# Seven products per group in another order, in a Winograd-form fp32 kernel on TensorE

## The reference

```python
# x (2048, 512), beta (1024, 8, 512), W (1024, 512), b (1024,)
s   = einsum('bn,hln->bhl', x, beta)
ssq = einsum('bn,hln->bhl', x * x, beta * beta)
out = 0.5 * sum(s * s - ssq, axis=-1) + x @ W.T + b      # (2048, 1024)
```

## Time and profile before

| what | value |
|---|---|
| three runs, us | 785.6, 786.31, 787.71 (median 786.31) |
| the profiled execution, its own time | 786.93 us |
| its span, first to last instruction | 785.1 us |
| granted TensorE clock, mean | 0.996 |
| PE (TensorE matmul) busy | 774.1 us, 99% |
| DVE (VectorE) busy | 564.3 us, 72% |
| ACT (ScalarE) busy | 401.2 us, 51% |
| POOL (GpSimd) busy | 366.0 us, 47% |
| DMA queue, share of 16 engines | 51.6% |

### The profile page before, as it was taken

One profiled execution on the slowest core, in us unless ns is written; L12 is line 12 of the kernel. 1 busy time (PEld: TensorE's weight loads), 2 busy tenths in 40 slices (PEclk: granted clock), 3 DMA queues, 4 the chain that ended last, 5 costly groups with the idle time before them and its releaser, 6 DMA issues. The chain is left out here.

```text
span 785.1 us, 9688 instructions
## 1 busy us (share of the span) xinstructions
PE 774.1 (99%) x3382; PEld 635.4 (81%) x3382; DVE 564.3 (72%) x582; ACT 401.2 (51%) x500; POOL 366.0 (47%) x328
## 2 busy tenths in 40 slices
PE   9999999899999999999999999999999999999998
PEld 6887878688888888888888888888888888887886
DVE  6899379965666567667757665776577657688995
ACT  6565356454555555465545554555455546552330
POOL 0133177336454644454455445653564366343443
PEclk9999999899999999999999999999999999999999
DMA  8696944075634462456146604661456155627933
GB/s 346 241 363 265 357 146 157 14 269 186 221 121 147 138 225 100 148 183 223 51 148 214 215 28 148 214 215 34 155 207 215 34 192 207 229 77 307 391 122 151
DMA packets 64017, 145.35 MB, mean 185 GB/s; under 512 B 4832, under 2 KB 41696, under 8 KB 61664
## 3 DMA queue, kind: packets, MB, share of 16 engines
q1 hardware_dynamic: 63968, 144.72, 51.6%
HBM read 102.76 MB, written 41.94 MB: 184 GB/s over the span
## 5 line engine op out<-in xcount | busy, mean ns | idle before, releaser
L441 PE MATMUL bank<-t_hi,s_hi 128*128 128x512 f32 x1108 | 433.1, 391 | 5.3 <-ACT r L611 4.2
L445 PE MATMUL bank<-t_lo,s_hi 128*128 128x512 f32 x1116 | 435.4, 390 | 0.0
L447 PE MATMUL bank<-t_hi,s_lo 128*128 128x512 f32 x1108 | 432.1, 390 | 0.0
L441 PEld LDWEIGHTS bank<-t_hi,s_hi 128*128 128x128 f32 x1108 | 208.7, 188 | 51.4 <-ACT r L611 5.5
L445 PEld LDWEIGHTS bank<-t_lo,s_hi 128*128 128x128 f32 x1116 | 210.3, 188 | 43.4
L447 PEld LDWEIGHTS bank<-t_hi,s_lo 128*128 128x128 f32 x1108 | 208.7, 188 | 43.5
L969 POOL TENSOR_TENSOR r<-r 128x512 f32<-128x512 f32 x70 | 96.3, 1376 | 182.9 <-ACT r L617 178.8
L965 POOL TENSOR_TENSOR acc<-acc,bias_all 128x128 f32<-128x128 f32 x128 | 64.9, 528 | 179.7 <-DMA acc<-acc_kept 179.6
L823 DVE TENSOR_REDUCE sums<-cs 128x256 f32<-128x2048 f32 x64 | 146.0, 2281 | 2.0 <-ACT cs L633 1.6
L808 DVE TENSOR_TENSOR cs<-bank,r 128x512 f32<-128x512 f32 x70 | 48.3, 690 | 111.7 <-PE bank L447 111.5
L605 ACT COPY r<-bank 128x512 f32<-128x512 f32 x78 | 45.9, 588 | 160.7 <-PE bank L447 160.7
(11 more groups left out here) (58 smaller groups left out, 333.0 us busy)
## 6 DMA issues: line engine op xcount, KB each, us to landing
s_hi<-s_hi_kept SPq DMA_DIRECT2D x30, 896.0 KB, 5.1
s_lo<-s_lo_kept SPq DMA_DIRECT2D x30, 896.0 KB, 6.9
t_lo_in<-beta_p SPq DMA_DIRECT2D x16, 1024.0 KB, 7.2
s_lo_in<-x_p SPq DMA_DIRECT2D x17, 512.0 KB, 5.8
acc_kept<-cs SPq DMA_DIRECT2D x16, 512.0 KB, 5.2
acc<-acc_kept SPq DMA_DIRECT2D x64, 128.0 KB, 5.4
acc_kept<-acc SPq DMA_DIRECT2D x64, 128.0 KB, 1.8
s_hi_kept<-s_hi SPq DMA_DIRECT2D x8, 896.0 KB, 5.9
```

Source lines behind the costliest of these rows:

```text
L441: nc.tensor.matmul(to, s_hi[:, slot, s_op, cols], hi[:, k, :], start=start, stop=False, skip_group_check=True)
L445: nc.tensor.matmul(to, s_hi[:, slot, s_op, cols], lo[:, k, :], start=False, stop=False, skip_group_check=True)
L447: return nc.tensor.matmul(to, s_lo[:, slot, s_op, cols], hi[:, k, :], start=False, stop=stop, skip_group_check=True)
```

## The change

The products of a group come in the order P5, P7, P1, P6, P3, P4, P2. Every other engine's row is written to match:

- ScalarE: c11 of the group before first, then r5, `square_rest`, r7, r1; `split_s` of x goes to the end of the group in which its sums are made.
- VectorE: c21 in its own group, behind `sum_s`; `split_s` and `sum_rows` ahead of `add_r2`. In passes 1 to 9 `sum_s` stays between r2 or c12 and what follows. The sums for group 15 move from group 12 to 13, its split from 13 to 14.
- POOL: the bias is added behind c22 instead of ahead of r57, in one instruction of 128x256.
- SP: waits for P4 become waits for P2, and the halves are stored in the order in which they are done.
- Last pass, from group 73 on: VectorE adds P5 and P7 from their banks straight to the fourth quarter of f (`p5_taken`, `p7_taken`), and P3 and P4 wait for these; r5 and r7 are not made there. POOL adds r2 to three quarters of f. Group 72 still copies r5 and r7.

```diff
@@ SUMMED_IN, SPLIT_IN
-SUMMED_IN.update({PAIRS + 6: PAIRS + 3, PAIRS + 7: PAIRS + 4, FIRST_Q: FIRST_Q - 3, FIRST_Q + 1: FIRST_Q - 2})
+SUMMED_IN.update({PAIRS + 6: PAIRS + 3, FIRST_Q: FIRST_Q - 3, FIRST_Q + 1: FIRST_Q - 2})
-SPLIT_IN.update({PAIRS + 6: PAIRS + 4, PAIRS + 7: PAIRS + 5, FIRST_Q: FIRST_Q - 2, FIRST_Q + 1: FIRST_Q - 1})
+SPLIT_IN.update({PAIRS + 6: PAIRS + 4, FIRST_Q: FIRST_Q - 2, FIRST_Q + 1: FIRST_Q - 1})
@@ store_rows (SP)
-                sp.wait_ge(o11_added, i + 1)
-                sp.wait_ge(c12_added, count(g))
-                sp.dma_start(out[rows:rows + P, :], f[:, 0, :]).then_inc(stored, 16)
-                sp.wait_ge(o22_added, i + 1)
-                sp.dma_start(out[rows + P:rows + 2 * P, COLS:], f[:, 1, COLS:]).then_inc(stored, 16)
-                sp.wait_ge(c21_added, count(g))
-                sp.dma_start(out[rows + P:rows + 2 * P, 0:COLS], f[:, 1, 0:COLS]).then_inc(stored, 16)
+                sp.wait_ge(c12_added, count(g))
+                sp.dma_start(out[rows:rows + P, COLS:], f[:, 0, COLS:]).then_inc(stored, 16)
+                sp.wait_ge(c21_added, count(g))
+                sp.wait_ge(o22_added, i + 1)
+                sp.dma_start(out[rows + P:rows + 2 * P, :], f[:, 1, :]).then_inc(stored, 16)
+                sp.wait_ge(o11_added, i + 1)
+                sp.dma_start(out[rows:rows + P, 0:COLS], f[:, 0, 0:COLS]).then_inc(stored, 16)
@@ tensor
+                wait_bank(g, BANK_E)
+                whole(g, BANK_E, S1, T1, True).then_inc(p5_made, 1)
+                wait_bank(g, BANK_D)
+                whole(g, BANK_D, S3, T3, True).then_inc(p7_made, 1)
                 wait_bank(g, BANK_A)
                 whole(g, BANK_A, A11, B11, True).then_inc(p1_made, 1)
                 wait_bank(g, BANK_B)
                 whole(g, BANK_B, S2, T2, True).then_inc(p6_made, 1)
...
+                if g <= FIRST_Q:
+                    pe.wait_ge(r5_copied, count(g))
+                else:
+                    pe.wait_ge(p5_taken, g - FIRST_Q)
+                whole(g, BANK_E, S4, B22, False).then_inc(p3_made, 1)
+                if g <= FIRST_Q:
+                    pe.wait_ge(r7_copied, count(g))
+                else:
+                    pe.wait_ge(p7_taken, g - FIRST_Q)
+                whole(g, BANK_D, A22, T4, False).then_inc(p4_made, 1)
                 pe.wait_ge(r1_copied, count(g))
                 whole(g, BANK_A, A12, B21, False).then_inc(p2_made, 1)
@@ scalar
             for g in range(DIRECT, FIRST_Q):
-                copy_r1(g)
+                if g > DIRECT:
+                    take_c11(g - 1)
+                copy_r5(g)
                 if g > FIRST_MAIN:
                     square_rest(g - 1)
-                if g > DIRECT:
-                    for other in groups_for(SPLIT_IN, g):
-                        split_s(other)
-                copy_r5(g)
                 copy_r7(g)
+                copy_r1(g)
                 for other in groups_for(SUMMED_IN, g):
                     if other >= FIRST_Q:
                         square_x(other)
-                take_c11(g)
                 for s in steps_in(g):
                     step(g // PAIRS + 1, s)
+                for other in groups_for(SUMMED_IN, g):
+                    split_s(other)
@@ vector, main passes
             for g in range(FIRST_MAIN, FIRST_Q):
-                add_c21(g - 1)
                 for s in steps_in(g - 1):
                     step((g - 1) // PAIRS + 1, s)
-                add_r2(g)
+                for other in groups_for(SPLIT_IN, g):
+                    split_s(other)
                 if g > FIRST_MAIN:
                     sum_rows(g - 1)
-                for other in groups_for(SPLIT_IN, g):
-                    split_s(other)
+                add_r2(g)
                 add_c12(g)
                 for other in groups_for(SUMMED_IN, g):
                     sum_s(other)
+                add_c21(g)
@@ vector, last pass
                 if i:
-                    add_o21(g - 1)
+                    dve.wait_ge(f_loaded[i], 16)
+                    dve.wait_ge(p5_made, count(g))
+                    nc.vector.tensor_tensor(f[:, 1, COLS:], bank(g, BANK_E), f[:, 1, COLS:], ALU.add
+                                            ).then_inc(p5_taken, 1)
+                    dve.wait_ge(p7_made, count(g))
+                    dve.wait_ge(p5_taken, i)
+                    nc.vector.tensor_tensor(f[:, 1, COLS:], bank(g, BANK_D), f[:, 1, COLS:], ALU.add
+                                            ).then_inc(p7_taken, 1)
                     for other in groups_for(SPLIT_IN, g):
                         split_s(other)
...
                 add_r2(g)
...
-                nc.vector.tensor_tensor(r5[:, :], bank(g, BANK_E), r2[:, :], ALU.add).then_inc(r25_added, 1)
...
-                nc.vector.tensor_tensor(r5[:, :], bank(g, BANK_D), r5[:, :], ALU.add).then_inc(r257_added, 1)
@@ gpsimd, last pass
                 nc.gpsimd.tensor_tensor(f[:, 0, COLS:], f[:, 0, COLS:], r2[:, :], ALU.add).then_inc(f12_added, 1)
                 nc.gpsimd.tensor_tensor(f[:, 1, 0:COLS], f[:, 1, 0:COLS], r2[:, :], ALU.add
                                         ).then_inc(f21_added, 1)
-                pool.wait_ge(r257_added, i + 1)
-                nc.gpsimd.tensor_tensor(f[:, 1, COLS:], f[:, 1, COLS:], r5[:, :], ALU.add).then_inc(o22_added, 1)
+                if i:
+                    pool.wait_ge(p7_taken, i)
...
+                nc.gpsimd.tensor_tensor(f[:, 1, COLS:], f[:, 1, COLS:], r2[:, :], ALU.add).then_inc(o22_added, 1)
```

More of the change, by code:

```diff
@@ L215, in fm_layer @@
         acc_added = sem("acc_added")
-        r25_added = sem("r25_added")
-        r257_added = sem("r257_added")
+        p5_taken = sem("p5_taken")
+        p7_taken = sem("p7_taken")
+        f22_added = sem("f22_added")
         o11_added = sem("o11_added")
@@ L680, in _ @@
                         square_x(other)
-                take_c11(g)
                 for s in steps_in(g):
                     step(g // PAIRS + 1, s)
+                for other in groups_for(SUMMED_IN, g):
+                    split_s(other)
+            take_c11(FIRST_Q - 1)
+            copy_r5(FIRST_Q)
+            square_rest(FIRST_Q - 1)
+            copy_r7(FIRST_Q)
             for g in range(FIRST_Q, GROUPS):
                 copy_r1(g)
-                if g == FIRST_Q:
-                    square_rest(g - 1)
                 for other in groups_for(SUMMED_IN, g):
@@ L871, in _ @@
                     split_s(other)
+                for other in groups_for(SUMMED_IN, g):
+                    sum_s(other)
                 add_r2(g)
```

101 lines of the change are left out of this document (36 added, 65 removed).

## The result

The changed kernel took **781.52 us** (median of 5 runs, 780.87 to 781.91) against 786.31 us for the kernel before on the same chip (5 runs, 785.07 to 787.71): a ratio of 0.9937, 95% interval 0.992 to 0.9954. Forecast were 781.5 us and a range from rival A's lower form, 776.9, up to 784.0. A repetition on another chip gave 781.69 against 786.65, 0.9943 (0.9922 to 0.9963).

What follows compares the result with a forecast made beforehand. TensorE was taken to bound the kernel, with 9.97 us of pauses and slow clock to win; -9.97 + 0.56 + 4.08 + 0.55 = -4.78 us off the 786.31 us median gave 781.5 us, range 776.9 to 784.0.

Steps and rivals of the forecast that it cites:

- rival A: Last pass stays TensorE's, POOL catching two pieces of sum_s: 777.4 us; lower form, without group 71's pause, 776.9; chance 0.2.
- Up to group 72: Groups 2 to 71: earlier pauses and slow stretch go, one new pause comes; -8.66 + 0.56 us.
- Group 71's pause: Late square_rest and copy of P7 hold P4 of group 71 by 0.45, with the restart +0.56 us.
- Group 13's cause: Late square_rest delayed P5's copy and P3: 3.45 us over the pitch, then 2.79 more at half clock.
- part (1) of the theory: Gain up to group 72 comes from ScalarE's and VectorE's rows around preparing x, and group 9's later bias addition.
- rival B: sum_s meets a long POOL operation, takes 4.57, holds groups 12, 14, 70 and 71: +3.1, 784.6 us; chance 0.12.
- The bias: POOL's bias addition no longer ahead of r57 in group 8, so late acc loads stop causing group 9's pause.
- The last pass: From group 73, three POOL additions released by r2 alternate with sum_s: +4.08 us of pauses; the earlier 1.31 go.
- the period: VectorE's time per group in the last pass: 10.47 us against TensorE's 9.52.
- Tail: Last store leaves 0.28 later with 256 KB more just ahead of it: +0.55 us, between 0 and 1.2.
- Rival C: Late load of x holds TensorE in groups 70 and 71: 788.7 us at one place, 795.9 at two; chance 0.05.
- The added wait for the loaded rows: Ahead of P5's addition in the last pass, costed at nothing because the loads leave up to 4 us earlier.

Runs made afterwards that it cites:

- experiment 6: Changed kernel with the old tables: sums for group 15 made in group 12 again, its split in 13; 783.18 us against 786.55, 0.9958.
- experiment 7: Kernel before with only the sums for group 15 moved to group 13 and its split to 14; 781.87 us against 786.55, 0.9934.
- Experiment 5: Changed kernel with POOL's bias addition, still one instruction, put back ahead of r57; 783.31 us against 785.75, 0.9967.
- experiment 1: Changed kernel with sum_s ahead of r2 in the last pass and x squared ahead of the copy of P1; 777.33 us against 785.75, 0.9891.
- experiment 2: Changed kernel with POOL's third addition in the last pass held until VectorE's addition of P3 is done; 777.48 us against 785.75, 0.9888.
- experiment 3: Changed kernel with each POOL addition of the last pass done as two of 128x256; 778.23 us against 786.55, 0.9893.
- Experiment 4: Changed kernel up to group 71, with the last pass on all engines as before; 779.15 us against 785.75, 0.9907.
- experiment 8: Kernel before with the moved sums and split for group 15 and the one-instruction bias addition behind c22; 780.96 us against 786.65, 0.993.

## Why the prediction was right, point by point

- **Up to group 72**, forecast -8.10, profiled -8.51. The pauses of groups 6, 9 and 13 and the slow stretch are gone, as forecast; the split for group 6 ended at 63.99 (forecast 62.8 to 64). Group 71's pause was forecast at 0.56 and is 0.13: square_rest and the copy of P7 ended 0.4 earlier than worked out, since `sum_s` in 69 and 70 lasted 2.60 (684.89 to 687.49 in 70) where the prediction let it run 2.8 to 2.95. The place and the instruction were right, the size was not.
- **Group 13's cause.** The prediction told the three edits there (c21 earlier, copy of P5 ahead of square_rest, the sums moved) in one breath, with one price. Experiments 6 and 7 part them: the moved sums alone take 5.8 of the 6.5 us, the new order alone about 4. So the larger cause is the one that the prediction named last and that part (1) of the theory did not name. Their effects don't add: in before the slow stretch took 2.8 of the 6.5, and with either edit the clock stayed at 1.00. The reason for the table's weight stood in the earlier trace rows: 4.57 us for a `sum_s` that takes 1.47 alone. The prediction used that number only as the price of rival B and did not ask which instruction of POOL stood behind it; it was the 128x1024 sum (136.96 to 139.54).
- **The bias.** The prediction called the late load of acc the cause of group 9's pause and said that it goes. Experiment 5 shows it, at 1.9 us in group 9; in before the pause and its restart cost 0.77 + 0.39 - 0.23 + 0.11, about 1.
- **The last pass**, forecast +4.08 - 1.31 = +2.77, profiled +2.08. The mechanism is shown by experiments 1 to 3: three edits that have in common only that they cut the number or the length of POOL's turns inside `sum_s` each remove all of 3.39. The term that was off is the period, 10.35 for 10.47: the instruction behind `sum_s` starts 5.23 behind r2's start (722.03 to 727.26), worked out were 5.33. Five periods make 0.6 of the 0.69 missing, and group 74's pause is 0.03 for 0.2.
- **Tail**, forecast +0.55, profiled +0.50; the last store at 10.69 (forecast 10.7).
- **Rival A** (the last pass stays TensorE's) would be true with one more wait on POOL, experiment 2: 777.48 measured, 777.4 worked out. The margin was narrower than the prediction had it: by its own bound of 9.68 the changed kernel is 0.67 over and not 0.8, and in experiment 2 `sum_s` is 3.65 and not 3.0, the period 9.38 and not 8.8. **Rival B** shows in experiment 6 rather than in the change: a long POOL instruction in front of `sum_s`. **Rival C** did not come, but the cover is thin. ScalarE did wait for x in group 69 (1.31 us idle, the load landing at 672.48, 6.0 after its issue), and the square was done at 673.56, 0.43 before VectorE wanted it. By these rows, as an estimate, a landing time of 6.4 us would begin to delay `sum_s`, and as the copy of P7 in group 70 ended at 5.38, due 6.80, some 7.8 would begin to hold TensorE, not 9 as the prediction had it. No run here had such a load, so rival C's price stays untested.
- **The added wait for the loaded rows** ahead of P5's addition cost nothing in the changed kernel. Experiment 4 shows the same load reaching TensorE by way of POOL and a VectorE instruction.
- **That the total came out to 0.02 us is luck, though the mechanism held.** The terms of the trace give -5.93 for the profiled pair, where the forecast had -4.78; the medians give -4.79 here and -4.96 in the repetition. The forecast's terms gained 1.15 too little, and the medians show 1.14 less than the terms.
- **Where the missing us lies, as far as the record tells.** The prediction took the pauses of one profiled execution of before off the median. That execution is 0.62 above its median, and it had a long stretch at the lower clock (mean clock 0.996). Of the 39 executions of before beside the experiments, 6 had a mean clock of 1.00 and took 784.3 us on average, 20 had 0.998 and 786.0, 11 had 0.996 and 787.5 (the other two 0.997 and 0.994, 787.6 and 790.7). By these clocks, 0.998 or more in 26 of 39, most of them lost less to the clock than the 2.79 us of the earlier trace rows. None of them was traced, so whether their pause in group 13 was shorter too stays open. The expectations of experiments 4 and 8, 777.7 and 779.4, took the whole loss off the median as well, and both came out too low (779.15 and 780.96). The other half is on the side of after: its profiled execution is the fastest of its five, 0.65 below the median. T2 lies between 28.2 and 29.8 in the nine executions of the new order, although no edit among them touches what is ahead of it, and the idle time ahead of P3 of group 9 was 0.77 in one execution of the old order and 1.41 in another (experiment 7).
